# New turn strings, and shorter norm statistics, reciprocal roots and score maxima on VectorE, in a fused sampling, attention and experts kernel

## Time and profile before

| | |
|---|---|
| median of 3 runs | 4566.16 us |
| the profiled execution, first to last instruction | 6851.9 us |
| PE, matmul busy | 4265.1 us |
| DVE (VectorE) busy | 3165.0 us |
| POOL (GpSimd) busy | 3077.1 us |
| ACT (ScalarE) busy | 2222.4 us |
| TensorE clock granted, mean | 0.734 of full speed |

### The profile page before, as it was taken

The page is one execution under the profiler, slowest core; times in us unless marked ns, Lnnn a source line. Parts: engine busy times, 40 slices in busy tenths (PEclk is TensorE's granted clock), DMA queues, the critical chain, the costliest instruction groups (busy, mean ns, idle before and its releaser), DMA issues.

```text
span 6851.9 us, 83914 instructions
## 1 busy us (share of the span) xinstructions
PE 4265.1 (62%) x26592; PEld 3681.7 (54%) x26592; DVE 3165.0 (46%) x10220; ACT 2222.4 (32%) x5378; POOL 3077.1 (45%) x3089
## 2 busy tenths in 40 slices
PE   3566765657566575665766667565765757656664
PEld 2555655646455464654656556454654646545543
DVE  1455445354454534545354544534545454544521
ACT  1333332323333332332333323333333333322321
POOL 2554454444534445354454544445344444545331
PEclk9777777777767776786777767777777777767765
DMA  6754443635536354353545536254353545433122
GB/s 194 216 154 136 145 135 115 177 96 157 148 103 189 86 174 119 118 165 94 175 118 160 144 106 190 84 176 119 118 164 93 175 113 152 138 106 89 54 59 67
DMA packets 938637, 911.33 MB, mean 133 GB/s; under 512 B 121306, under 2 KB 822362, under 8 KB 938072
## 3 DMA queue, kind: packets, MB, share of 16 engines
q1 hardware_dynamic: 805768, 598.22, 30.0%
q0 software_dynamic: 132432, 307.74, 15.5%
HBM read 583.69 MB, written 323.53 MB: 132 GB/s over the span
## 4 chain that ended last, share of the span: by engine, by line
another core or an unknown queue 31%; PE 29%; DVE 14%; issue 13%; ACT 10%; SPq 1%; DMA 1%; POOL 0%; DVEq 0%; POOLq 0%; ACTq 0%
PE ps L867 4%; PE ps L881 4%; PE ps L1024 3%; PE ps L1032 3%; PE ps L812 3%; PE ps L964 3%; PE ps L942 2%; ACT rows L1048 2%; ACT xm L1128 2%; DVE prod L1229 1%; PE ps L954 1%; PE ps L1006 1%; PE ps L823 1%; ACT kv_sb L1048 1%
## 5 line engine op out<-in xcount | busy, mean ns | idle before, releaser
L758 POOL DMA_INDIRECT gath<-table,idx x2048 | 2048.2, 1000 | 2909.6 <-issue 1211.3
L881 PE MATMUL ps<-w_kv,samp_t 128*128 128x128 f32 x4096 | 702.9, 323 | 166.6 <-issue 88.1
L867 PE MATMUL ps<-const,prod 128*128 128x128 f32 x4096 | 684.4, 322 | 168.8 <-issue 81.7
L964 PE MATMUL ps<-v_sb,probs_t 128*128 128x64 f32 x2880 | 455.2, 307 | 476.9 <-issue 223.1
L881 PEld LDWEIGHTS ps<-w_kv,samp_t 128*128 128x128 f32 x4096 | 637.0, 234 | 201.0 <-issue 130.5
L964 PEld LDWEIGHTS ps<-v_sb,probs_t 128*128 128x128 f32 x2880 | 442.9, 229 | 544.2 <-issue 303.5
L867 PEld LDWEIGHTS ps<-const,prod 128*128 128x128 f32 x4096 | 596.5, 172 | 202.7 <-issue 152.4
L774 POOL DMA_INDIRECT xs_d<-xm,row x512 | 525.9, 1027 | 392.7 <-DVE row L1229 231.6
L790 POOL DMA_INDIRECT ya<-ys_d,row x512 | 493.4, 964 | 454.4 <-DMA ys_d<-yx 268.6
L1229 DVE TENSOR_TENSOR prod<-gath,corner_w 128x1024 f32<-128x1024 f32 x512 | 619.9, 1219 | 159.3 <-remote 70.6
L942 PE MATMUL ps<-k_t,q_t 128*128 128x512 f32 (+3 forms) x960 | 479.7, 592 | 181.6 <-ACT v_sb L1048 76.5
(11 more groups left out here) (171 smaller groups left out, 6593.0 us busy)
## 6 DMA issues: line engine op xcount, KB each, us to landing
table<-rows SPq DMA_DIRECT2D x224, 1024.0 KB
fm<-in_x SPq DMA_DIRECT2D x256, 512.0 KB
wx<-w_d SPq DMA_DIRECT2D x768, 128.0 KB
gath<-table,idx POOLq DMA_INDIRECT x2048
wx<-w_d SPq DMA_DIRECT2D x64, 512.0 KB
table<-rows SPq DMA_DIRECT2D x32, 960.0 KB
xg<-xs_d SPq DMA_DIRECT2D x192, 130.0 KB
ys_d<-yx SPq DMA_DIRECT2D x192, 128.0 KB
```

The source lines that it names most:

```text
L758: pool.indirect_dma_start(out=gath[:, n % NG, p, :], out_offset=None, in_=tables[par], in_offset=bass.IndirectOffsetOnAxis(ap=idx[:, par, ...
L867: last = pe.matmul(bank(0, p * P, p * P + P), prod[h][:, (p * 2 + dx) * P:(p * 2 + dx + 1) * P], ident, is_transpose=True, start=(dx == 0) ...
L881: last = pe.matmul(bank(1, p * P, p * P + P), samp_t[n % 2][:, (4 * h + p) * P:(4 * h + p + 1) * P], w_kv[:], start=True, stop=True)
L964: last = pe.matmul(bank(7, (i % 8) * C, (i % 8) * C + C), probs_t[n % 3][:, (k % 4) * P:(k % 4) * P + P], v_sb[:, k, :], start=(k == 0), s ...
```

## The change

It replaces all strings of `TURNS` and `LAST` (the tensor and scalar strings, and `LAST`, are left out below). For the norms it reads `bn_stats`' six numbers of a tile directly: it has a mean and a sum of squared deviations for each half of the 64 channels, and the change sums the halves of all nine tiles with one reduction and corrects the variance by the difference of the half means. `rsqrt` becomes one of two longer steps of four instructions, 10 instructions in all. In the score maximum the scale of -1/8 goes into the fused instruction, which now takes the minimum, so the extra multiplication falls away, and `soft` waits for the chunk itself where there is one chunk. The first image norm now waits on a semaphore `bn_ok` of the last token tile's statistics. `off_hidden` has one part fewer, so one letter g fewer in VectorE's string.

```diff
-RSQRT_SEED = float(0x5F3759DF)
+RSQRT_STEP = 0.375
+RSQRT_SEED = float(0x5DCB741A)
 MASKED = -1.0e30
 HALF_UP = 0.49609375
-LOWEST = -3.4e38
+HIGHEST = 3.4e38
...
-    return order + [*[("off_hidden", ())] * 24, ("off_exp", ()), *[("off_gelu", ())] * 3, ("off_turn", ()),
+    return order + [*[("off_hidden", ())] * 23, ("off_exp", ()), *[("off_gelu", ())] * 3, ("off_turn", ()),
...
 TURNS = {
+    "sync":
+        "gghgggxxxxxxxxgxxggxxgxxggxxxxgggggggggehggggxxxxxxxxxxe",
+    "gpsimd":
+        "pppppppffffffffffffffffpffffffffffffffffpppccccccccccccccccccccccccccccccccppppp",
...
     "vector":
-        "wawaaxawwaaaaaaaaaaawvvxwwvvaaxvvwaavvvvvvxavavxaavwaawaavxvvvavawxwavvvaxaavvvwwvvavvvvaxvvvvaawaav"
-        "waaavvvavavvaawaaaaaaaaaaaaaaaavwvvvvvvveveeeaaavaeeeeaaawwavvavvveaeveeeevaaaraavvevvwaewrvraraeara"
-        "rvavvaaaaaaaraavevrrrrvvrxrwwvrgggggggggggvgeeegxggggggeeeeegggwegvaxvgaexvvexaaagvaggxxaevaaaxxavav"
-        "vvwxaxxaavaevvvxavxeeeeeeeggeeeaeeewxaeevevgeeeaeeeveexgxaagxxageexxexgxxgavxavwaaxvavvvxvvawvvvvvvv"
-        "avxxawvxvvavwaxaaaaaaaawaaaaaavvvvvvxvvvvvvvvaaaaaaaaxaaaavvaaa",
-    "gpsimd":
-        "pppppppffffffffffffffffpppffffffffffffffffccccccccccccccccccccccccccccccccpppppp",
-    "sync":
-        "ggxxgxxgxgxxxggxgxgxxhxgxxxgggggggggggxxgehgxgxxxexxxxxx",
+        "waawaaaaaaaaaaaaawxwwvwvvvvxwvwvvvwxwvvvvvvvxwwvvvvvvxvvvvvvwvvxvvwvvvvvxvvvvvvvvaxvwvvaxawvwavaavvw"
+        "avaaaawaaavavavaavvvvvavaaaweeeaeaaaeeeaeeeaeaeeeeeeeeeeeeeeeavavvvvveeawaaaaaaaaaaaaaaawewvvwveaaaa"
+        "aaeaaaaaaeraaaaaaaaaaaaawwrarrrrrrrrrraaaarrvvxvwwxxxgxxggggggggggggxgxxwxgggggggggxaaxxxgggvxaxxxve"
+        "evxvxaxaaaxaaaaxaaagggggggagaaaaxaaaxxxvxxxavaaavavvveewavavvevvvvveevxvvewwvvvxvveevavavevvxvvveeee"
+        "eeeeeeeevvaaaaaaaaaaaaaaaavevvvvveevvvvvaaaaaavaaaaaavaaavvvvv",
 }
...
             def soft(pair, par, b, i):
-                act.wait_ge(*s_max.rise(pair, ST_N * b + i + 1))
+                if key_chunks(i) == 1:
+                    act.wait_ge(*s_rd.rise(pair, KEY_CHUNKS * b + i + 1))
+                else:
+                    act.wait_ge(*s_max.rise(pair, LONG * b + i + 1 - (ST_N - LONG)))
                 n = (i + 1) * P
                 act.activation(probs[i % 2][:, 0:n], probs[i % 2][:, 0:n], ACT.Exp,
-                               bias=att[:, 1, i:i + 1], scale=ATT_SCALE,
+                               bias=att[:, 1, i:i + 1], scale=-1.0,
                                accum_out=att[:, 2, i:i + 1]).then_inc(s_exp.sem, 1)
...
-            def rsqrt(r, v, t, h):
+            def rsqrt(r, v, t):
 
                 step(ts(t.bitcast(I32), v.bitcast(I32), 1, ALU.logical_shift_right))
-                step(ts(h, v, -0.5, ALU.mult))
                 yield
                 settle()
                 step(ts(r.bitcast(I32), t.bitcast(I32), -1.0, ALU.mult, RSQRT_SEED, ALU.add))
                 yield
                 settle()
-                for _ in range(3):
-                    step(tt(t, r, r, ALU.mult))
+                for c in (RSQRT_STEP ** -4, RSQRT_STEP ** -2):
+                    step(stt(t, r, c, r, ALU.mult, ALU.mult))
                     yield
                     settle()
-                    step(tt(t, t, h, ALU.mult))
+                    step(tt(t, t, v, ALU.mult))
                     yield
                     settle()
-                    step(stt(r, t, 1.5, r, ALU.add, ALU.mult))
+                    step(stt(t, t, -10.0 / 3.0, t, ALU.add, ALU.mult))
+                    yield
+                    settle()
+                    step(stt(r, t, 5.0, r, ALU.add, ALU.mult))
                     yield
                     settle()
 
...
-                yield from rsqrt(st16[:, 2], st16[:, 1], st16[:, 3], st16[:, 4])
+                yield from rsqrt(st16[:, 2], st16[:, 1], st16[:, 3])
...
-                step(dve.bn_stats(bn[:, t, :], (h0[:, b], h1[:, par, b], out_sb)[k][:, t, :]))
+                last = dve.bn_stats(bn[:, t, :], (h0[:, b], h1[:, par, b], out_sb)[k][:, t, :])
+                if k == 0 and t == QT_N - 1:
+                    last.then_inc(bn_ok.sem, 1)
+                else:
+                    step(last)
+
+            def halves(k):
+
+                bn, ab = (bn6, bn6_1, bn6_e)[k], ln9_e if k == 2 else ln9
+                return bn[:].rearrange("p t (h f) -> p t f h", f=3)[:, :, 1:3, :], ab
 
             def moments(pair, par, b, k):
                 settle()
+                if k == 0:
+                    dve.wait_ge(*bn_ok.rise(pair, b + 1))
                 dve.sem_inc(dve_gate, 1)
-                for t in range(ST_N):
-                    step(dve.bn_aggr((mv_e if k == 2 else mv)[:, t, :], (bn6, bn6_1, bn6_e)[k][:, t, :]))
+                two, ab = halves(k)
+                step(red(ab[:, 0:2].rearrange("p f t -> p t f"), two))
+                step(tt(ab[:, 2], two[:, :, 0, 0], two[:, :, 0, 1], ALU.subtract))
 
             def scale(pair, par, b, k):
                 settle()
-                ab, m = (ln9_e, mv_e) if k == 2 else (ln9, mv)
-                step(ts(ab[:, 0], m[:, :, 1], EPS, ALU.add))
-                yield
-                settle()
-                yield from rsqrt(ab[:, 3], ab[:, 0], ab[:, 1], ab[:, 2])
-                stt(ab[:, 4], m[:, :, 0], -1.0, ab[:, 3], ALU.mult, ALU.mult).then_inc(
+                _, ab = halves(k)
+                own(stt(ab[:, 2], ab[:, 2], 0.25, ab[:, 2], ALU.mult, ALU.mult))
+                step(stt(ab[:, 1], ab[:, 1], 1.0 / C, ab[:, 2], ALU.mult, ALU.add))
+                yield
+                settle()
+                step(ts(ab[:, 1], ab[:, 1], EPS, ALU.add))
+                yield
+                settle()
+                yield from rsqrt(ab[:, 3], ab[:, 1], ab[:, 2])
+                stt(ab[:, 4], ab[:, 0], -0.5, ab[:, 3], ALU.mult, ALU.mult).then_inc(
                     end_ab.sem if k == 2 else ln_ab.sem, 1)
 
             def score_max(pair, par, b, i, c):
...
                 end = c == key_chunks(i) - 1
                 plus = const[:, MASK + P - m:MASK + P] if end else zero.to_broadcast([P, m])
                 one = end and c == 0
-                most = att[:, 0, i:i + 1] if one else att_m[:, n:n + 1]
+                least = att[:, 1, i:i + 1] if one else att_m[:, n:n + 1]
                 dve.sem_inc(dve_gate, 1)
                 dve.tensor_tensor_reduce(out=probs[i % 2][:, a:a + m], in0=bank(4 + n % 2, 0, m), in1=plus,
-                                         scale=1.0, scalar=LOWEST, op0=ALU.add, op1=ALU.max,
-                                         accum_out=most).then_inc(s_rd.sem, 1)
-                if end:
+                                         scale=-ATT_SCALE, scalar=HIGHEST, op0=ALU.add, op1=ALU.min,
+                                         accum_out=least).then_inc(s_rd.sem, 1)
+                if end and c:
                     dve.wait_ge(*s_rd.rise(pair, KEY_CHUNKS * b + n + 1))
-                    if c:
-                        own(red(att[:, 0, i:i + 1], att_m[:, n - c:n + 1], ALU.max))
-                    ts(att[:, 1, i:i + 1], att[:, 0, i:i + 1], -ATT_SCALE, ALU.mult).then_inc(s_max.sem, 1)
+                    red(att[:, 1, i:i + 1], att_m[:, n - c:n + 1], ALU.min).then_inc(s_max.sem, 1)
```

More of the change, by code:

```diff
@@ L114 @@
 KEY_CHUNKS = first_chunk(ST_N)
+LONG = sum(key_chunks(i) > 1 for i in range(ST_N))
 def token_stages():
@@ L241 @@
 TURNS = {
+    "sync":
+        "gghgggxxxxxxxxgxxggxxgxxggxxxxgggggggggehggggxxxxxxxxxxe",
+    "gpsimd":
+        "pppppppffffffffffffffffpffffffffffffffffpppccccccccccccccccccccccccccccccccppppp",
     "tensor":
-        "xxtxtkxtkxgtgakgatxgaaaxgagxssxtkgqxsatxgsqxsgkgxqtxgkgsxgagxagxtxsgsqgxkgtxgaxgkgxqsxgqsxtqkxtagsqa"
-        "xtxkgsagqtgkgaqtgssqagsqakqgaaqaqagagkggtgaagkagkgagtgkggtgkgtgkgtgrgkgtgxgkgtgxkgxagaxgaaatasxsksqs"
-        "axqtsaxqksxaqsgtxsqasgqxkaastqsxsqktkxaxaqxkxqsaqxssqatxaqkqtqxakaxaatxtxkxktaxkaaxaxx",
+        "xgxgxgtgktgktxgatxkxtkxtxtxtkxtxkxgtxgkxgkxgtxgkxgxgtxgakxgaxgkgaxgkaxgsxgtxgaxgsxssqksqgtqgktgakgts"
+        "gaqkgatssqgassqgassqgatqgaqssqgqgakqgasgakgaqgaqgaqatagkgtgkgtaaktagtagkgtgkggrgtgtxgxgxgxgaaxgtaxax"
+        "axaxssxssxqgqxsxqgxaxasaqssxsxsqaqqaqassqassqakqaskqtaqtxqaxkxkxqtxkxktxaxtxakakaakaaa",
@@ L246 @@
     "scalar":
-        "xxttkxtagkgatxgaaaaagtaxgagvkxstqsxgkxgtsgvqgxqkgxggstgxgkxgtgsxqvgxkgsggxqtxkqtqkgxtvxsqggktggqtsqg"
-        "vkqggqskqgqqggtggaagvkaagkagatvgkggtgkggtgkgtvgaktgggkgtgxgkvagxagagatagakxaaeeeavstsqxgqskqtssqxgqv"
-        "kqkxtsqstkexqtkeeqxsvqqqxstkvqqktqvxxtkxtkxaavktaakaaxvxa",
+        "xgxggtgktaagktxaatxgkvtkxtxttkxvxtkgtxgkxvgkgtxgvkxggtxagkxgvagkgaxkgaxvggstxgaxgsqskqgtqgktgkgstvgq"
+        "kgstqgsqgsvqgtqgqsqggqkgqgskgqgeqeeqvgtgkgtgkaataaagtagktgkgtgagggtgtxgxgaagxgaaagaxaaxagsxsqgqsxvqx"
@@ L250 @@
+        "sqsxsqqqqsqskqkqtsqvtqxkqxvktxktxkvtxqxtkvkeeeakaaavkaaav",
     "vector":
[L251 to L254 removed]
@@ L260 @@
+        "evxvxaxaaaxaaaaxaaagggggggagaaaaxaaaxxxvxxxavaaavavvveewavavvevvvvveevxvvewwvvvxvveevavavevvxvvveeee"
```

(25 more changed lines are left out.)

12 lines of the change are left out of this document (4 added, 8 removed).

## The result

The changed kernel takes 4595.55 us (median of 5 runs, 4593.8 to 4613.13) against 4566.56 us for the kernel before (5 runs, 4557.32 to 4577.35): a ratio of 1.0072, 95% interval 1.0055 to 1.0089. The forecast was 4468 us and faster.

What follows compares the result with a forecast made beforehand. POOL was taken as the fullest engine, 3989 of 4566 us. From 4566 us, 95 us of POOL waits and 3 us of DVE steps in the tail were subtracted, giving 4468 us; range 4375 to 4640 us.

Steps and rivals of the forecast that it cites:

- Standstill that comes with being profiled: In the profiled execution's chain, 2124 us on another core or unknown queue, taken as profiling's effect; 4728 us left without it.
- 302 us for the tail: What follows POOL's gathers: 437 us in the profile, scaled by the ratio 4728 to 6852.
- 275 us of waits between first and last gather: POOL's remaining idle time in that stretch of 4141 us, 17 us a pair, taken as what a better order can win.
- shares of these waits by name: POOL's listed waits: weigh's slots and the indices were given 1576 of 1808 us, 87%.
- gain of 95 us: On POOL, new strings give slot and index waits room; 40% of 239 us won, bounds nothing and 239 us.
- POOL as the fullest engine: All 3072 indirect transfers: 3067 us plus 922 us of issue, 3989 us, 87% of 4566 us.
- 249 us for a shorter run: POOL transfers stretched by DVE through the shared port: 166 us in all, 249 us if overlaps become denser.
- The distances of letters: Turn strings: gaps between writing and waiting letters, as shares of each engine's period; indices 2% to 9%, most slots more room.
- Rival C: Slower, 4669 us, chance 0.22: DVE stops at weigh 12 for late data; POOL loses 5 us at group 4 each period.
- Rival B: Order doesn't matter, PE and ACT chains pace the waits, only DVE's steps count: 4549 us, chance 0.20.
- The edits: DVE's norms, off_hidden and score maximum: about 83 us less DVE work, 17 us of it reaching the end.
- DVE busy near 3082 us: Sign expected in the profile after: DVE's busy time at 3165 less 83 us.

Runs made afterwards that it cites:

- disturbed set: Runs, no edit, in which every version took half as long again, profiled or not: the kernel before 6744 to 6882 us, against 4557 to 4583 us undisturbed.

## Why the prediction was wrong, step by step

- **"Standstill that comes with being profiled."** This is the step that failed first. The standstill belonged to the disturbed set, not to the profiler, and what was worked out from it fell: the 302 us for the tail (336.7 measured), the 275 us of waits between first and last gather (105.5 measured), and the shares of these waits by name. The forecast's gain of 95 us was 40% of 239 us that were not there. I wrote that I would scale nothing that is a wait, and took the waits' shares from that same list.
- **POOL as the fullest engine** held, and held better than I thought: 4009.7 of 4115.2 us between first and last gather. To win 95 us there, an order would have had to remove nine tenths of the 105.5 us of waits. The transfers were 3117 us, where I put 2973: the mean was 1.044 us for a gather, not 1.000. Over the median of 0.946 us they lose 303 us, where the forecast had 166. The Trainium skill, SBUF — State Buffer, "Who interferes with whom", calls the port pair that VectorE and GpSimd share an exclusive lock; from that I had worked out 249 us for a shorter run, and kept it out of the sum. The direction agrees: the transfers did lose more in the shorter run.
- **The distances of letters** told the direction and not the size. Group 9 had 3%, and its 54.6 us of waits went when it got 8%. Group 4 went from -1 to -2%, and 57.7 us of waits came: 67.1 us instead of 9.4. Before, the group at 3% waited in 11 periods and the one at -1% in one. I listed both, and let only the gain into the forecast.
- **What the fetch waits for** is missing from the prediction. I moved the fetch from 50 to 42% in one sentence, and did not ask what the first fetch waits for. ys_d was set aside as a wait of the tail. SyncE's string was read for loads and store, and not for table 2 ahead of the last two expert stores: 80.5 us in 13 periods.
- **Rival C** had the right sign. One of its two terms came about: 5 us of POOL in full at group 4 (measured 5.2 us a time, 13 times). The other, VectorE stopping for late gathers, did not: its wait for them is no larger after (148.2 us) than in the undisturbed run of before (161.8). The wait for ys_d was missing from it, and its price was too high.
- **Rival B**, that the order doesn't matter, was near in time for another reason: the room was used, and new waits of the same queue took its place.
- **The edits** were sized well: 83 us of DVE forecast, 80.7 measured on the old strings; 17 us of time forecast, 15 measured. The split holds too: the norms' own instructions keep DVE busy for 36.4 us less (294.7 to 258.3; 35 forecast), and the 288 multiplications that fell away took 44.2 us (45 forecast). The sign "DVE busy near 3082 us" still failed for the changed kernel (3151.9 us), since the new strings gave 79 us back. On the new strings the edits win nothing that can be told; that the wait for SyncE's stores holds POOL there is the likely reason, not a tested one.
- **LAST** I did not price at all; it wins 23 us.

## What to carry to other kernels

Before a sum is built on a profile, its span has to be that of the timed runs; a trace that is 50% longer can't say which waits exist, whatever is subtracted from it. In a kernel that runs from hand-made orders, add up the fullest engine from its first to its last instruction (transfers, issue, waits). Where waits are 2 to 3%, as here, a new order has little to win there and much to lose; most of the gain here lay in the tail. Read a new order for each queue, the DMA queue's too: two pairs of letters of SyncE's string were worth 35 us. And where an order takes room at one letter and gives it at another, both go into the forecast.
